# Latent attention: unread products beside the maxima where two units meet, and the turned sums straight ahead of the next two rows of maxima

## The reference, cut to what matters

```python
q = (x @ Wq.T) in heads;  latent = layernorm(x @ Wdkv.T)
k, v = latent @ Wuk.T, latent @ Wuv.T in heads;  q, k = apply_rope(q), apply_rope(k)
scores = einsum('bhqd,bhkd->bhqk', q, k) / sqrt(HEAD_DIM), causal
attn = softmax(scores)
out = einsum('bhqk,bhkd->bhqd', attn, v) @ Wo.T
```

## Time and profile before

| | us |
|---|---|
| median of 3 runs | 1664.8 |
| lowest, highest | 1656.7, 1669.15 |
| the profiled execution | 1654.05 |
| its span (first to last instruction) | 1652.3 |

### The profile page before, as it was taken

One profiled execution on the slowest core, in us unless ns is written; L12 is line 12 of the kernel. 1 busy time (PEld: TensorE's weight loads), 2 busy tenths in 40 slices (PEclk: granted clock), 3 DMA queues, 4 the chain that ended last, 5 costly groups with the idle time before them and its releaser, 6 DMA issues. The chain is left out here.

```text
span 1652.3 us, 36830 instructions
## 1 busy us (share of the span) xinstructions
PE 1229.8 (74%) x14007; PEld 648.0 (39%) x14007; DVE 1169.2 (71%) x2634; ACT 953.3 (58%) x1539; POOL 582.1 (35%) x1039
## 2 busy tenths in 40 slices
PE   2755564466667778999998576776878899998848
PEld 2753454366442222223333265653222222233337
DVE  4348698735768889997775355576888999786235
ACT  2226775322345678888887442244666788878622
POOL 2430078146654331221111564575341111111236
PEclk9977676678569999999999788757999999999869
DMA  9252000021000000000010152000000000000023
GB/s 256 74 175 90 1 4 3 24 67 55 1 3 2 1 2 1 1 2 9 21 28 27 51 138 60 2 1 1 1 2 1 2 1 1 2 1 2 1 76 40
DMA packets 56799, 50.77 MB, mean 31 GB/s; under 512 B 7921, under 2 KB 52066, under 8 KB 56178
## 3 DMA queue, kind: packets, MB, share of 16 engines
q1 hardware_dynamic: 48818, 37.77, 8.2%
q0 software_dynamic: 6864, 9.55, 2.3%
q10 hardware_dynamic: 944, 1.10, 0.2%
HBM read 36.16 MB, written 21.35 MB: 35 GB/s over the span
## 5 line engine op out<-in xcount | busy, mean ns | idle before, releaser
L1902 DVE TENSOR_REDUCE arena<-psum 128x1 f32<-128x512 f32 (+4 forms) x1152 | 681.0, 654 | 141.6 <-PE psum L1708 96.9
L1843 ACT ACTIVATE arena<-psum 128x1024 f32<-128x1024 f32 (+3 forms) x640 | 557.9, 899 | 180.8 <-PE psum L1730 172.0
L1746 PE MATMUL psum<-arena 128*9 128x256 f32 (+2 forms) x4352 | 339.1, 388 | 0.8 <-POOL arena L1962 0.8
L1708 PE MATMUL psum<-arena 64*128 64x128 bf16 (+3 forms) x1664 | 224.9, 319 | 96.4 <-DVE arena L1902 86.1
L1730 PE MATMUL psum<-arena 64*128 64x512 bf16 (+3 forms) x1280 | 228.8, 357 | 22.8 <-ACT arena L1843 15.5
L1962 POOL TENSOR_SCALAR_AFFINE_SELECT arena<-arena 128x256 f32<-128x256 f32 x256 | 103.0, 406 | 369.0 <-ACT arena L1843 365.6
L1708 PEld LDWEIGHTS psum<-arena 64*128 64x128 bf16 x1664 | 69.9, 96 | 274.2 <-DVE arena L1902 233.4
L1730 PEld LDWEIGHTS psum<-arena 64*128 64x128 bf16 x1280 | 63.3, 94 | 175.6 <-ACT arena L1843 77.1
L1746 PEld LDWEIGHTS psum<-arena 128*9 128x9 f32 x4352 | 67.8, 89 | 152.5 <-issue 118.2
L1940 POOL CAST arena<-arena 128x16 bf16<-128x16 f32 x64 | 16.3, 255 | 284.3 <-DVE arena L1907 282.1
L698 ACT ACTIVATE small<-psum,YT 128x128 f32<-128x128 f32 x168 | 52.5, 364 | 93.4 <-PE psum L651 93.2
(11 more groups left out here) (368 smaller groups left out, 2015.1 us busy)
## 6 DMA issues: line engine op xcount, KB each, us to landing
regions<-sorted_rows SPq DMA_DIRECT2D x11, 741.8 KB, 14.1
big_w<-in_w SPq DMA_DIRECT2D x2, 2048.0 KB, 20.3
arena<-taps SPq DMA_DIRECT2D x16, 256.0 KB, 3.4
arena<-taps SPq DMA_DIRECT2D x4, 1024.0 KB, 10.8
ACCn<-regions SPq DMA_DIRECT2D x48, 64.5 KB, 1.8
ACCn<-made_rows SPq DMA_DIRECT2D x12, 256.0 KB, 3.8
w<-in_w SPq DMA_DIRECT2D x2, 1024.0 KB
sorted_rows<-arena SPq DMA_DIRECT2D x1, 1483.5 KB, 14.5
```

Source lines behind the costliest of these rows:

```text
L1708: mm = pe.matmul(psum[:, bank_of(("max", (v, m + r))), at:at + w], plain_q[v % 2][rows, a, i * P:(i + 1) * P], keys[rows, 2 * hq + a, key: ...
L1746: mm = pe.matmul(psum[32 * hh:32 * hh + 9, O_BANK, lo:hi], values[:, tile_of(v, j), 4 * hq + hh, :], prob[(t + hh // 2) % N_PROB][:, hh % ...
L1843: act.activation(prob[t % N_PROB][:, :, off:GW], both, ACT.Exp, scale=INV_SQRT_HD).then_inc(a_got, 1)
L1902: dve.tensor_reduce(place, rows, AX.X, ALU.max).then_inc(a_max_got, 1)
```

## The change

Three edits, of which two add instructions and one moves them.

1. `thin_pairs` goes over the events and finds the maxima that stand at a place with no weighing: ahead of the first weighing of all, and between the last weighing of a unit and the first of the next. Ahead of each such pair, behind its wait for the bank, `keep_warm` puts one matmul of 512 columns into the bank that the pair is about to write. There are 52 such pairs in each attention: units 0 and 1 with 6 each and 2 of unit 2 ahead of the first weighing (14), then 5, 3, 4, 3, 3, 3, 3, 3, 2, 3, 2, 3 at the meets after units 0 to 11, and 1 after unit 12.
2. `turn_out` waits for its bank first, puts two such matmuls into it, and only then waits for ScalarE's copy of the sums.
3. `plan` puts `out` just ahead of an even number, so straight ahead of a pair of maxima, but not ahead of the fourth half tile. It moves ahead of one pair (two rows of maxima) after units 0 and 2 to 9, and besides, or otherwise, ahead of a score; after unit 15 it stays.

```diff
@@ plan
-                places += [(after[2] - 0.2, "take", v), (after[4] - 0.2, "out", v)]
+                places += [(after[2] - 0.2, "take", v), (max(int(after[4] - 0.2) // 2 * 2 - 0.01, after[3] - 0.2), "out", v)]
@@ attention_pe
+                def thin_pairs():
+
+                    thin, found = True, set()
+                    for kind, x in events:
+                        if kind == "weigh":
+                            thin = x[1] == TILES_OF[x[0]] - 1 and x[2] == 1
+                        elif kind == "max" and thin:
+                            found.add(x)
+                    return found
+
+                thin = thin_pairs()
+
@@ maxima
                     bank_free(("max", (v, m + 1)))
+                    if (v, m) in thin:
+                        keep_warm(bank_of(("max", (v, m))), 1)
                     at = 0
@@ turn_out
                 def turn_out(event):
+                    bank_free(event)
+                    keep_warm(bank_of(event), 2)
                     pe.wait_ge(a_took, units + event[1] + 1)
-                    bank_free(event)
```

## The result

| | before | changed |
|---|---|---|
| median | 1665.09 us of 4 runs | 1691.29 us of 4 runs |
| lowest, highest | 1656.7, 1669.15 | 1687.05, 1694.44 |
| the profiled execution | 1654.05 us | 1691.88 us |

The ratio is 1.016, with a 95% interval of 1.0117 to 1.0208: the changed kernel is slower by 19 to 35 us. The prediction was 1672 us with a range of 1654 to 1688, so the time lies above it.

The account below looks back on a forecast made before the run. VectorE's reads were taken to bound the meets, in a loop with TensorE's maxima. Meets 11.2, starts 8.8 and clock -4 made +16 us, 1670 on the profiled execution, set at 1672 us for the runs; range 1654 to 1688.

Parts of the forecast that it names:

- The loop: At the meets, TensorE's maxima and VectorE's reads loop over three banks with about 0.04 us of slack in 1.20.
- Rival C: Products covered by other waits at most meets, only the start pays: 0 us, 1654 to 1665; chance 0.10.
- The price of a product at full clock: One added 512-column matmul takes 0.22 us, so about 0.19 us at a meet after the loop's slack.
- The move: Turned sums ahead of a pair at nine meets give back about 0.25 us each, -2.2 us an attention.
- Products at the turns: The two products before each turn are covered by VectorE's reads; otherwise each would cost 0.22 us.
- The starts: 14 products in series at the low clock, 5.9 us, less 1.0 and 0.5 for the clock: 4.4 us an attention.
- The clock at the meets: Low-clock stretches at meets cost 7.7 us; products bring back half, -4 us.
- thin meets: Meets of units where TensorE has little work; they cost the clock sometimes, not always.
- meets, products and move: At the meets of both attentions: 7.0 - 2.2 + 0.6 + 0.2 = 5.6 us each, 11.2 us together.
- Rival B: Clock rises no earlier, low stretches stay, each start product costs 0.42: +23 us, 1677 or 1688; chance 0.25.
- Rival A: Starts and all meets run at full clock: -3 us, 1651 or 1660 on the median's scale; chance 0.23.
- Scale: Profiled 1654.05 us plus 16 gives 1670; of the 10.8 us to the median not all was added: 1672.

Follow-up runs that it names:

- e1: Kernel before plus one unread product ahead of each of the 52 pairs, none at turns, nothing moved: 1686.85 us, ratio 1.0173.
- e3: Changed kernel with the product ahead of each pair split into two of 64 rows: 1682.87 us, ratio 1.0142.
- e4: Changed kernel without the two products before each turn: 1683.64 us, one run.
- e8: Changed kernel with two products ahead of each pair in place of one: 1708.07 us, one run.
- e2: Kernel before with only the turned sums moved ahead of the pair, no products: 1653.06 us, ratio 0.9981.
- e6: Kernel before plus three unread products ahead of each of the 14 start pairs, nothing else: 1677.4 us, one run.
- e7: Kernel before plus half-array products ahead of 68 pairs behind each unit's first three weighings, none at meets, starts or turns: 1691.37 us, one run.
- e9: Kernel before with turned sums moved only after units 0 and 2 to 9, two products at turns after units 12 to 15: 1659.47 us, ratio 0.9999.
- e10: Kernel before with each unit's first weighing in two column halves, result incomplete, only times read: 1666.65 us, ratio 1.0034.
- e11: Kernel before with first weighings in two column halves and turned sums moved, no products, result incomplete: 1654.83 us, ratio 0.9981.
- e12b: Kernel before with first weighings in halves, whole result computed, turned sums moved only after units 0 and 2 to 7: 1654.62 us, ratio 0.9963.
- e13b: Kernel before with first weighings in two column halves, whole result computed, nothing moved: 1660.63 us, ratio 1.0001.

## Why the prediction was wrong, step by step

**The loop: right.** VectorE's reads bound the meets and TensorE's product stands in series in the loop. Its slack hid even less than the 0.04 us: the loop grew by 0.30 for a product of 0.32, and three half-array products on top of the move cost 0.64, 0.21 each. The gaps of about 0.2 before pairs are there (0.21 at 1407.27), and the first one grew from 0.21 to 0.53. Rival C, covered products, had nothing.

**The price of a product at full clock: the step that failed.** The prediction read "0.23 us; I take 0.22" from a pair of maxima followed by a score, and took it for a whole-array product followed by a pair. Both rows of that reading are 64-row matmuls; the product is a 128-row one. It costs 0.32 (1406.52 to 1406.84), of which 0.10 is the switch, as the half-array run (0.22, unit 40.00) and the double product (0.53, unit 40.96) show. The trace of before held the price, in the other direction: behind the pair of 512 columns at 1334.13 a weighing, which uses all 128 rows, starts after 0.31 us, where a score starts after 0.23.

```profile
1334.44 0.41 PE L1746 MATMUL psum<-arena 128*9 128x128 f32 x8
```

Put into the prediction's own working, 3 x 0.10 on its +0.36 gives +0.66 for a unit, which is what was measured, and without the switch (the half-array run) it is +0.35. 37 such products would make 3.7 us more an attention, 7.4 for both; the middles of the half-array run and of the changed kernel, the clock taken out, are 8.7 us apart.

**The move: right in size by itself, and it gave next to nothing beside the products.** -0.25 was forecast for a unit and -0.29 measured with the move alone. But between the run with products at pairs alone (40.36) and the changed kernel (40.31) it is -0.05, since there the gap after the sums had already come down to 0.40. That the unit comes out at +0.66 either way (-0.29 and 3 x 0.32, or 3 x 0.24 and -0.05) hides it. The wait for the copy after unit 10 was too small in the prediction, 1.01 us with the move alone, but by the last weighings it costs about 0.1.

**Products at the turns: right**, covered (unit 40.31 with and without). The single gap of 0.35 after the sums came as two, 0.38 and 0.16.

**The starts: too low.** Forecast 4.4 each, measured 6.2 and 5.7. A product in series costs 0.54 at the low clock (506.41 to the pair at 506.95; the second attention's first one, 1143.42 to 1143.96, likewise), not 0.42, the switch again:

```profile
506.41 0.61 PE L188 MATMUL psum<-counts,identb 128*128 128x512 bf16 x1 [0.54 <-DVE arena L1917]
506.95 0.61 PE L1722 MATMUL psum<-arena 64*128 64x512 bf16 x2
```

14 x 0.54 is 7.6, and with the prediction's own -1.0 and -0.5 for the clock 6.1. The first start has indeed gained 3.4 us at the full clock, the second one too. It is the misread price again: with half-array products the two starts together took 9.1 us more, where 8.8 was forecast.

**The clock at the meets: too high, and the low stretches went elsewhere.** "Between nothing and all of it I take half" was -4 us. In the profiled executions nothing came back: the two middles together have 45.4 us at the low clock where they had 40.1, at 0.25 a loss of 1.3 us. Executions differ much in this, so all profiled ones must be asked: with products at the meets (the changed kernel, e1, e3, e4, e8) it is 45.4, 23.9, 30.8, 31.7 and 20.5 us, 30.5 on average; without them (before, e2, e6, e7, e9 to e11, e12b and e13b) it is 40.1, 35.7, 30.7, 31.8, 29.9, 38.8, 43.8, 50.1 and 40.1, 37.9 on average. That is 7 us less, or about 2 us of time, from groups that overlap. So the products may bring back a quarter of the 7.7 us, hardly half. Where the stretches begin says more. A meet runs here from a unit's last weighing to the first one of the next. Of the eight stretches in the middles of before (the prediction counted seven, one of 3.4 us too few) five begin in a meet, two in mid-unit and one just behind a first weighing; of the nine in the changed kernel two begin in a meet, six in mid-unit and one just behind a first weighing. Over the same two groups of profiled executions, the stretches that begin in meets make 26 us on average without products there (17 to 38) and 14 with them (7 to 24), those that begin elsewhere 7 and 14. So the prediction's ground, thin meets, was sound for most of the low time, and the products may well have lifted the clock there; but of the 12 us that went at the meets 7 came back elsewhere, for which the prediction had no term. Whether the products bring these stretches on is not shown. The longest one, 10.2 us from 1232.2, begins 7.5 us behind the sums of unit 2, where the new unit's small tiles go by and no product stands:

```profile
1232.81 0.61 PE L1722 MATMUL psum<-arena 64*128 64x512 bf16 x2 [0.89 <-DVE arena L1917]
...
1238.90 0.50 PE L1722 MATMUL psum<-arena 64*128 64x384 bf16 x2 [0.88 <-DVE arena L1917]
```

The first stretch of the earlier trace rows, at 554.9, is such a place too, 6.4 us behind the sums of unit 2, though the prediction called all seven "at meets of units".

**The sum.** In us for both attentions, on the profiled executions; the clock in the middles is the time at the low clock at 0.25, and the meets are what is left of the middles:

| step | forecast | half-array products | changed kernel |
|---|---|---|---|
| meets, products and move | 11.2 | 12.1 | 20.8 |
| starts | 8.8 | 9.1 | 11.9 |
| clock in the middles | -4 | -2.4 | +1.3 |
| sum | +16 | +18.8 | +34.0 |

With the price that the prediction had used made true, its terms come out within 2 us each. Of the gap of 18 us in the changed kernel the switch makes 8.7 at the meets and 2.8 at the starts, the clock in the middles 5.3; the rest is 1.2. The clock's part is that of one execution and partly chance. The medians of these two kernels are 8.4 us apart (1682.87 and 1691.29), which their scatter does not tell from the 11.5. Rival B's condition, no clock regained, came about at the meets and not at the starts, and its 1688 on the median's scale was too low by the switch. Rival A, a clock that holds, did not come about with one product a pair: the starts were at the low clock for 25.2 of 28.6 us and 20.2 of 27.1.

**Scale.** The prediction added only 2 of the 10.8 us between the profiled execution and the median, on the ground that slower runs have more to win back. Little was won back. With all of it the forecast would have been 1681, so this choice makes 8.8 of the 19.3 us by which 1672 missed the median of 1691.3, from the same belief in the clock. On the medians the change cost 19 to 35 us.

## What to carry to other kernels

Price an added instruction from a row in which the same kind of neighbour stands behind it, and not from a row with the same number of columns: on TensorE look at the load of weights of the next matmul, and whether it lies under the one ahead or starts with its own. Filler that stands behind the wait for a buffer is in series with the engine that empties it, and pays in full unless the slack of that loop is larger; put it where the engine waits for something else, as at the turns, where it cost nothing. Before filler is put in to hold a clock, hold the times of the low stretches against the places it will stand at, and look afterwards for new ones elsewhere. And when something is moved, do not measure by it: take a mark that both kernels have in the same place.

## What the runs showed that was not expected

- **A switch from whole-array to half-array matmuls costs TensorE 0.10 us at full clock and 0.12 at the low one** (0.32 against 0.22 per product; 0.54 against 0.42), and one the other way about 0.09 (0.31 against 0.22 or 0.23, from a pair to a weighing, which is float32 besides).
- **A read by VectorE lasts 0.68 us, but the next one in a row starts after 0.60**, so every wait costs 0.08 or 0.09 us of lost overlap besides its own length (two reads 1.29, six in a row 3.68).
- **Lifting the clock at a start cost at least what it gave**: three products a pair leave 4.3 and 1.8 us at the low clock, and the start is as long as with one (27.93 beside 28.05 us from first pair to first weighing); two took 25.2 and 29.3 us in the two attentions, none 22.4 and 21.4.
- **The stretch between the attentions, which no version touches, takes either about 195 or about 207 us.** Taken to the first pair, in the profiled executions of before, the changed kernel and the versions e1, e2, e4, e9 and e11 it is 195.2 to 196.5 us with 93 to 103 us at the low clock; in those of e3, e6, e7, e8, e10, e12b and e13b it is 205.0 to 208.8 with 117 to 128. The difference is larger than all that the gaining versions gained, and it hides them: the split alone shows -6.6 us in its attentions and +12.2 there. Whether the version decides it or chance does stays open; the runs of one kernel, e12b's from 1646.99 to 1664.79, are farther apart than the two.
